# GpSimd weights and adds the two softmaxes of the second layer, with another order of TensorE's work in each step

## What is computed

```
scores = jnp.einsum('bhnd,bhmd->bhnm', q, k) / jnp.sqrt(D)      # D = 16
p = jax.nn.softmax(scores, axis=-1)
...
out1 = _attn(q[0], k[0], v)
out2 = _attn(q[1], k[1], v)
out = out1 - jnp.exp(lambda_p) * out2
h = _layernorm(h + out @ Wo + bo)
```

## Time and profile before

| | |
|---|---|
| three runs | 352.99, 356.2, 357.58 us; median 356.2 us |
| the profiled execution | 352.78 us, its span 351.0 us |
| TensorE busy, share of the span | 315.4 us, 90% |
| VectorE | 163.9 us, 47% |
| ScalarE | 89.2 us, 25% |
| GpSimd | 68.2 us, 19% |
| first loop (call 0), TensorE | 228.39 to 270.52 us |
| second loop (call 1), TensorE | 307.10 to 343.78 us |

### The profile page before, as it was taken

One profiled execution on the slowest core, in us unless ns is written; L12 is line 12 of the kernel. 1 busy time (PEld: TensorE's weight loads), 2 busy tenths in 40 slices (PEclk: granted clock), 3 DMA queues, 4 the chain that ended last, 5 costly groups with the idle time before them and its releaser, 6 DMA issues.

```text
span 351.0 us, 7357 instructions
## 1 busy us (share of the span) xinstructions
PE 315.4 (90%) x3090; PEld 257.6 (73%) x3090; DVE 163.9 (47%) x457; ACT 89.2 (25%) x206; POOL 68.2 (19%) x80
## 2 busy tenths in 40 slices
PE   8989598998799999999999898979999889799992
PEld 7855357874599999999999677845668748346771
DVE  0132247659312311111110297579997462766555
ACT  0022028340031222211111027512331122712230
POOL 8000000180524443443313140000001100000002
PEclk9999699898999999999999999898999999989998
DMA  7999400010238999899940400000000000000002
GB/s 295 379 296 302 110 4 1 18 54 2 55 111 273 285 306 313 292 274 290 309 163 34 140 2 0 0 2 4 3 2 3 0 0 2 0 2 3 2 0 70
DMA packets 12035, 38.59 MB, mean 110 GB/s; under 512 B 1786, under 2 KB 5754, under 8 KB 11771
## 3 DMA queue, kind: packets, MB, share of 16 engines
q1 hardware_dynamic: 10083, 34.20, 30.3%
q0 software_dynamic: 1920, 3.93, 3.7%
HBM read 34.93 MB, written 3.19 MB: 109 GB/s over the span
## 4 chain that ended last, share of the span: by engine, by line
PE 75%; DVE 13%; DMA 3%; ACT 3%; issue 3%; POOL 0%; SPq 0%; POOLq 0%; DVEq 0%; ACTq 0%
PE ps L738 11%; PE ps L497 8%; PE ps L726 8%; PE ps L727 8%; PE ps L530 5%; PE ps L817 4%; PE ps L778 3%; PE ps L770 3%; PE ps L555 2%; PE ps L795 2%; PE ps L556 2%; PE ps L611 2%; PE ps L805 2%; PE ps L570 2%; PE ps L828 2%
## 5 line engine op out<-in xcount | busy, mean ns | idle before, releaser
L438 POOL TENSOR_TENSOR rstd<-veps,neg_half 128x2 f32<-128x2 f32 (+1 forms) x16 | 10.6, 659 | 204.5 <-DVE veps L1172 204.5
L726 PE MATMUL ps<-xga,w1t 128*128 128x128 f32 x240 | 46.4, 274 | 0.0
L727 PE MATMUL ps<-xgb,w1u 65*128 65x128 f32 x240 | 46.4, 274 | 0.0
L1277 DVE COPY ys<-ps 128x192 f32<-128x192 f32 x20 | 7.2, 358 | 75.5 <-PE ps L738 75.5
L738 PE MATMUL ps<-w1t,hid 128*128 128x192 f32 x240 | 42.2, 326 | 0.0
L497 PE MATMUL ps<-w1a,consts 128*128 128x384 f32 x96 | 40.1, 550 | 0.0
L738 PEld LDWEIGHTS ps<-w1t,hid 128*128 128x128 f32 x240 | 38.6, 190 | 0.0
L1009 ACT ACTIVATE hid<-ps 128x768 f32<-128x768 f32 x20 | 16.2, 810 | 84.5 <-PE ps L727 84.5
L726 PEld LDWEIGHTS ps<-xga,w1t 128*128 128x128 f32 x240 | 36.3, 191 | 0.0
L727 PEld LDWEIGHTS ps<-xgb,w1u 65*128 65x128 f32 x240 | 36.3, 191 | 0.0
L461 POOL DMA_INDIRECT y_rows<-ys,to_row x20 | 20.8, 1039 | 56.8 <-DVE ys L1277 56.8
(11 more groups left out here) (224 smaller groups left out, 530.1 us busy)
## 6 DMA issues: line engine op xcount, KB each, us to landing
w1t<-in_wt SPq DMA_DIRECT2D x20, 960.0 KB
w1u<-in_wu SPq DMA_DIRECT2D x20, 240.0 KB
pat<-in_pat SPq DMA_DIRECT2D x6, 496.0 KB, 6.0
w1a<-in_w1a SPq DMA_DIRECT2D x1, 1322.0 KB
y<-y_rows SPq DMA_DIRECT2D x6, 192.0 KB, 3.3
w1b<-in_w1b SPq DMA_DIRECT2D x1, 835.2 KB
pos_bias<-in_pos_bias SPq DMA_DIRECT2D x1, 768.0 KB, 9.4
x_rows<-x_tok SPq DMA_DIRECT2D x3, 192.0 KB, 2.0
```

What stands on the lines that cost most here:

```text
L726: pe.matmul(out, w1t[:, b, 128 * k:128 * k + 128], xga[:, j % 2, :], start=True, stop=False)
L727: mm = pe.matmul(out, w1u[0:CB + 1, b, 128 * k:128 * k + 128], xgb[:, j % 2, :], start=False, stop=True)
```

## The change

Four things are edited.

1. In call 0, VectorE's `norm` ends with the small product L1353, which signals `p1_scaled`. The weighting of 128x600 elements and the two additions (128x200 and 128x100) are issued by GpSimd, group after group, between its copy of xt_hi and the third layernorm's `rsqrt`. Between its weighting and its additions GpSimd waits for its own semaphore `p1_weighted`. `p1_ready` is signalled by GpSimd.
2. In both calls the turn of group s-2 stands last in TensorE's step s, behind the products with the values and the projection.
3. In both calls `keep_busy` issues one 128x384 product in a step and not two.
4. Waits that go with it: ScalarE's exp of group s waits for `p1_ready` of s-2 (the buffer e1 is read by GpSimd), VectorE's `norm(g)` waits for `p1_ready` of g-2, GpSimd waits for the turn of g-2 before it writes the buffers of g. In call 1 VectorE goes on weighting by itself and waits for the turn of g-2 as before.

```
--- before.py
+++ after.py
@@ -275,6 +275,7 @@
         qk_ready, qk_act, qk_dve = sem("qk_ready"), sem("qk_act"), sem("qk_dve")
         s1_ready, s1_shifted, s1_exp = sem("s1_ready"), sem("s1_shifted"), sem("s1_exp")
         p1_ready, p1T_ready, p1T_done = sem("p1_ready"), sem("p1T_ready"), sem("p1T_done")
+        p1_scaled, p1_weighted = sem("p1_scaled"), sem("p1_weighted")
         o1_ready, o1_done = sem("o1_ready"), sem("o1_done")
         ce_ready, ha_ready, ha_done, hw_done = sem("ce_ready"), sem("ha_ready"), sem("ha_done"), sem("hw_done")
 
@@ -476,6 +477,20 @@
             pool.wait_ge(xb_done, 4)
             pool.tensor_copy(dense(xt_hi[CB:128, :]), unpadded(xpb[0:CB, :])).then_inc(x_twice, 1)
             pool.wait_ge(x_twice, 1)
+
+            def over(ap, n):
+
+                return bass.AP(tensor=ap.tensor, offset=ap.offset, ap=[list(d) for d in ap.ap] + [[0, n]])
+
+            for g in range(G):
+                pool.wait_ge(p1_scaled, g + 1)
+                if g >= 2:
+                    pool.wait_ge(p1T_ready, g - 1)
+                pool.tensor_tensor(e1[:, g % 2], e1[:, g % 2], over(st1[:, g % 2, 3, :], N), ALU.mult).then_inc(p1_weighted, 1)
+                pool.wait_ge(p1_weighted, g + 1)
+                sets = e1[:, g % 2].rearrange("p (a b c) m -> p a b c m", a=2, b=3)
+                pool.tensor_tensor(p1[:, g % 2, 0:2, :, 0:N], sets[:, :, 0], sets[:, :, 1], ALU.add)
+                pool.tensor_tensor(p1[:, g % 2, 2, :, 0:N], sets[:, 0, 2], sets[:, 1, 2], ALU.add).then_inc(p1_ready, 1)
             rsqrt(2)
             rsqrt(3)
 
@@ -833,16 +848,16 @@
                         pe.wait_ge(s1_shifted, G * call + step - 1)
                     if 0 < step < G + 2:
 
-                        keep_busy(2 * (step % 2), 2, 384)
+                        keep_busy(2 * (step % 2), 1, 384)
                     if step < G:
                         scores(step)
-                    if 2 <= step <= G + 1:
-                        turn(step - 2)
                     if step >= 3:
                         times_v(step - 3)
                     for t in range(TT):
                         if last_group(t) + 4 == step:
                             project(t)
+                    if 2 <= step <= G + 1:
+                        turn(step - 2)
                 for t in range(TT):
                     if last_group(t) + 4 > G + 2:
                         project(t)
@@ -1058,6 +1073,8 @@
                 for step in range(G + 3):
                     if step < G:
                         act.wait_ge(s1_shifted, G * call + step + 1)
+                        if step >= 2 or call:
+                            act.wait_ge(p1_ready, G * call + step - 1)
                         act.activation(e1[:, step % 2, 0:exps], s1[:, step % 2, 0:exps], ACT.Exp, scale=D1 ** -0.5).then_inc(s1_exp, 1)
                     if 2 <= step <= G + 1:
                         p1T_out(step - 2)
@@ -1344,18 +1361,15 @@
                     dve.wait_ge(s1_exp, n + 1)
                     e = e1[:, g % 2, 0:k, :]
                     total, inv, coef = (st1[:, g % 2, j, 0:k] for j in (1, 2, 3))
+                    if g >= 2 or call:
+                        dve.wait_ge(p1_ready, n - 1)
                     link(dve.tensor_reduce(total, e, AX.X, ALU.add))
                     link(dve.reciprocal(inv, total))
-                    if g >= 2 or call:
-                        dve.wait_ge(p1T_ready, n - 1)
                     p = p1[:, g % 2]
                     if two_sets:
-                        link(dve.tensor_tensor(coef, inv, lam[:, :, :, :].rearrange("p a b c -> p (a b c)"), ALU.mult))
-                        link(dve.tensor_tensor(e, e, over(coef, N), ALU.mult))
-                        blk = e.rearrange("p (a b c) m -> p a b c m", a=2, b=3)
-                        dve.tensor_tensor(p[:, 0:2, :, 0:N], blk[:, :, 0], blk[:, :, 1], ALU.add)
-                        dve.tensor_tensor(p[:, 2, :, 0:N], blk[:, 0, 2], blk[:, 1, 2], ALU.add).then_inc(p1_ready, 1)
+                        dve.tensor_tensor(coef, inv, lam[:, :, :, :].rearrange("p a b c -> p (a b c)"), ALU.mult).then_inc(p1_scaled, 1)
                     else:
+                        dve.wait_ge(p1T_ready, n - 1)
                         dve.tensor_tensor(view(p[:, 0, 0, 0:1], [[256, 2], [32, HQ], [1, N]]),
                                           e[:, 0:8].rearrange("p (a b) m -> p a b m", a=2),
                                           over(inv[:, 0:8].rearrange("p (a b) -> p a b", a=2), N), ALU.mult)
```

1 line of the change is left out of this document (added).

## The result

The changed kernel takes 350.26 us (median of 20 runs, 344.7 to 358.26), the kernel before 353.78 us (median of 20 runs, 349.87 to 359.37); the ratio is 0.9878 with a 95% interval of 0.9833 to 0.9922. The profiled execution of the changed kernel has a span of 345.0 us, 6.0 less than that of before.

A forecast was written before the change was run, and what follows sets the result against it. In the first loop VectorE bounds steps without a projection, TensorE those with; the second is TensorE's. Savings of 1.8 + 3.2 = 5.0 us from 352.8 give 347.8, ratio 0.986, carried over to 356.2 as 351 us; range 346 to 361.

The forecast's parts named there:

- GpSimd's price, 2.5 us: First loop: GpSimd's weighting and two additions for one group, 900 elements in three instructions with starts and signals, take 2.5 us.
- The row taken as nearest: GpSimd's copy at 1.47 ns an element, scaled by 1.5 for a second read to 2.2 ns, 2.0 us for 900.
- The lower and upper ends, 1.0 and 4.5: Bounds in us on GpSimd's work for a group: from a fill's rate, and from two copies' worth with dear starts.
- the slow rival: GpSimd takes 3.2 us or more a group and bounds the first loop; kernel even at about 3.7 us; chance 0.18.
- First turn at 7.8 us: First loop: the first turn begins 7.8 us after the first scores, when GpSimd is done, 0.4 later than before.
- The ring, 3.75 us a turn: First loop: product, scores, shift, half of norm, GpSimd, turn and signals take 7.5 us for two turns, 3.75 for one.
- the 1.2 for the clock: Start of the first loop: the lower clock lengthens turn (0.90 for 0.48) and product (1.39 for 0.65), 1.2 us added.
- TensorE's own step with a projection, put at 3.85: TensorE's step with a projection falls from 4.50 to 3.85 us once one product is taken out.
- 5.1 (0.48 + 1.1 + 1.1 + 2.4): End of the first loop: last turn, ScalarE's uncovered copies, values and three projections, in us.
- The second loop, 6.7 less 3.5: Nine products taken out save 6.7 us; 1.5 at the start and 2.0 at the end are given back, leaving 3.2.
- One low stretch at the start of each loop and none later: Expected sign: the granted clock falls to its lower level only at the start of each of the two loops.
- the rival that the clock doesn't hold: With one product half of the 17 steps run at the lower clock, adding 13 us, 364 carried over; chance 0.10.

The follow-up runs named there:

- e6: Changed kernel with GpSimd's 128x200 addition issued three times in a group, same result; median 360.4 us, two runs.
- e10: Changed kernel with four 128x384 products filling TensorE's wait before the first loop's first turn; ratio 0.9871, median 347.02 us.
- e12: Kernel before with one product in a step and four products filling the wait before the first loop's first turn; ratio 0.9933, median 349.31 us.
- e2: Kernel before with one product of keep_busy in a step and nothing else; ratio 0.9886, median 347.9 us.
- e1: Changed kernel with two products of keep_busy in a step again, in both loops; median 353.23 us.
- e8: Changed kernel with the turn ahead of values and projection in both loops; median 354.74 us, four runs.
- e3: Kernel before with the turn last in the step and nothing else; ratio 0.998, median 352.96 us.
- e9: Changed kernel run again, nothing edited; ratio 0.9834, median 349.04 us.
- e4: Changed kernel with the turn ahead of values and projection in the second loop only; ratio 0.9856, median 348.22 us.
- e7: Changed kernel without GpSimd's part: VectorE weights and adds, one product, turn last; 341.6 and 350.61 us, two runs.
- e5: Kernel of e4 with four 128x384 products filling TensorE's wait before the first loop's first turn; median 345.28 us.
- e11: Kernel of e5 with three more products filling TensorE's wait before the second loop's first scores; ratio 0.9729, median 342.42 us.

## Why the prediction held, and where it did not

The forecast was 351 us, 5.0 us less than before; measured are 350.26 and, by the medians, 3.5 less. The size is right by luck, for errors cancel in it: the path gave more than I had worked out (8.6 and not 5.0 us), and the clock, which the forecast held to be as before, took some 4.4 back. The 351 itself stands on the three runs' 356.2, which lies 2.4 above the 353.78 of twenty; the forecast's 0.986 of that would have been 348.8.

- **GpSimd's price, 2.5 us:** 2.4. The row taken as nearest (the copy, with three accesses for two) gave 2.2 ns an element and a start of 0.1 us; the two additions measured show 2.1 ns and a start of 0.19, and the multiplication, forecast at 1.4 us, took 1.20. The lower and upper ends, 1.0 and 4.5, were far from it, and e6 shows what the slow rival would have been: with two more additions the loop took 50.6 us. The estimate from the Trainium skill (GPSIMD Engine Reference, section "Elementwise — side-by-side cycle accounting") came to the same 2.5 us, and the trace agrees. Its advice to leave such work on VectorE ("Engine selection") is not borne out here: GpSimd is slower for each instruction (1.20 us for 0.78), but together with the late turn it is worth 2.4 us in the first loop at full clock (e10 for e12). Over all executions, read at one clock, no more than 0.6 us of that is seen.
- **First turn at 7.8 us:** 7.77.
- **The ring, 3.75 us a turn:** 26.3 us for seven turns (238.80 to 265.08) with a low stretch that the sum charged apart, where 26.2 and 1.2 stood: 1.1 us too dear. e10, whose loop has no low stretch, needs 25.2 (237.51 to 262.67), so the 1.2 for the clock was right and the mis-sized term is seven equal turns of 3.75. Its turns follow at 2.99, 4.23, 3.76, 3.70, 3.70, 3.47 and 3.31 us: the last two, in steps without scores, make 0.7 of the difference and the first two 0.3. TensorE's own step with a projection, put at 3.85, is 3.70, because the turn costs 0.33 and not 0.48 between the projection and the product. From the last turn to the end 4.7 us stand for 5.1 (0.48 + 1.1 + 1.1 + 2.4). Together the first loop saved 3.4 and not 1.8 us.
- **The second loop, 6.7 less 3.5:** the same 0.15 us in the four turns behind a projection, the first turn 4.9 us after the first scores where 5.2 were counted (6.7 less 1.47), and waits for ScalarE of 1.9 us (0.35, 0.29, 0.30, 0.94) where 2.9 were counted. It saved 5.2 and not 3.2 us.
- **"One low stretch at the start of each loop and none later":** so in both profiles of the changed kernel. The step that failed is the one taken from it, that the clock stays as it was and needs no term in the sum: over the executions the mean clock of 26 is 0.939 against 0.957 of 45. I had read the clock from one stretch of one profile and left it out of the sum; the rival that the clock doesn't hold had a chance of 0.10 and was thought of as all or nothing. What came is a loss of 4.4 us on average, not shown to lie in the loops' steps where the rival had it.
- **What of the change did it:** the prediction gave both new arrangements a share. e2 says that the product decides: it alone gives 0.9886, and at one clock 7.6 of the 8.2 us. With two products GpSimd and the order leave the median where it was (e1) and give some 2 us at one clock; GpSimd without the order loses most of the gain (e8); the order without GpSimd gives nothing that the runs can tell from noise (e3). Together and with one product they shorten the first loop by 2.4 us at full clock (e10's 37.6 against e12's 40.0), which the executions hardly show.

**What stays open:** how the thinner loops lower the mean clock. Its fall of 0.018 stands for 13 us more at the lower level in an execution of the changed kernel (0.018 x 2 x 350). Its two profiles have no more of it in the loops than the kernel before; what e9 has more lies 170 us ahead of them. The profiles of all kernels scatter in that stretch (24 to 56), from 6.8 us (before, e4, e8) over about 10 (most) to 16 (e7) and 24 (e6, e9), so one profile says little, and the profiles, one an execution, can't divide the difference. The difference itself is no chance: executions of one kernel scatter by 0.012, which leaves 0.003 for the difference of the two means. What was measured is that filling waits raises the mean, from 0.946 to 0.958 (e4, e5), from 0.939 to 0.952 (e9, e10) and to 0.969 (e11), but not from e2 to e12 (0.949, 0.947), so that filling a wait always helps is not shown.

## What to carry to other kernels

Work that only holds the clock costs its full length where TensorE is the path, and nothing where TensorE waits anyway (e5, e10, e11): try taking it out of the steps and putting it into the waits, and read the clock of many executions, since one profile may have drawn a good one. Moving work to an idle engine pays only if its chain then lies beside the busiest engine's work: follow the ring through every engine, and move the order with the work. Before crediting a bundle of edits, undo the smallest: one number out of four edits gave the gain of all four here, within the noise.

## What the runs showed of the hardware that was not expected

- GpSimd multiplied 128x600 by a broadcast operand in 1200 ns and added 128x200 in 607 and 128x100 in 396 ns: from the two additions 2.1 ns an element and some 0.19 us a start. With that start the multiplication, one of whose inputs is repeated over 25 elements, comes to 1.7 ns an element. VectorE took 0.78, 0.37 and 0.26 us for the same; its own instructions beside GpSimd's were no longer than before (0.78 and 0.77 us for 600 elements).
- At the lower clock narrow work slowed too, though less than wide: 48 records of scores 1.25 us for 0.85, 24 pairs of values up to 1.96 for 1.17, against 1.46 for 0.81 of the product.
- In e9 the lower level lasted for 24 us in which TensorE was busy 4.00 of 4 us for five stretches, the first two of them with 448-column products that took 1.70 us a pair; the first profile ran the same products, behind the same wait of 1.63 us, at 1.00 (28 to 32) in 0.92 us. Being busy did not bring the clock back there.
